# The row scalings of two layer norms moved from VectorE to ScalarE, in an attention and FFN block in float32

## The chip, the cores and the metric

One core of one Trainium2 chip runs the whole program. Its engines are TensorE (PE, matmuls into PSUM), VectorE (DVE), ScalarE (ACT), GpSimd (POOL) and SyncE (SP, which only issues transfers here). The metric is the time of one execution in device microseconds, the median over several. Lower is better.

## The reference, cut to what matters

```python
# x: (16, 16, 48, 128): 16 batches of 768 tokens with 128 channels, float32
def _ln(v, eps):                      # eps 1e-6 for the first norm, 1e-5 for the second
    m = jnp.mean(v, axis=-1, keepdims=True)
    s = jnp.var(v, axis=-1, keepdims=True)
    return (v - m) / jnp.sqrt(s + eps)

x = x + attention(_ln(x, 1e-6))       # 8 heads of 16, two relative position biases, causal in time, softmax over 768
t = x.reshape(16, 768, 128)
z = _ln(t, 1e-5)
top_p = top_k(softmax(z @ Wg), 2) / their_sum
for i in range(2):                    # every expert works on every token, scaled by top_p
    h = gelu(einsum("btd,edf->ebtf", z * top_p[..., i:i+1], W1) + b1)      # 8 experts, 512 wide
    out = out + einsum("ebtf,efd->btd", h, W2) + sum(b2)
x = t + out
```

## The kernel before, in words

A batch is 768 tokens, held as six tiles of 128 tokens (partitions) by 128 channels. For each batch the kernel computes the first norm, the transposes of its rows, query, key and value, the scores (twice: once for row maxima, once for the exponentials), the projection and residual, the second norm, the gate, and then the FFN.

The FFN is cut into 64 *units* a batch: 2 chunks of 384 tokens by 8 experts by 4 slices of the hidden width. A unit is a chain over all engines: three matmuls of TensorE into `zps` (L859 to L861), a product on VectorE (L691) that gives the second expert's input, two GELUs on ScalarE (L518 from PSUM, L519 from SBUF), the sum of both on GpSimd (L431), and six matmuls of TensorE into `acc` (L870). `zps` and `h0` have two buffers each. TensorE's matmuls of unit m wait for the first GELU of unit m - 2 (`h0_ready`), VectorE's product waits for the matmuls, and ScalarE's GELUs wait for the product (`z1_ready`).

The order of the work is written out by hand. `attention_plan` gives every attention step of the next batch a *slot* from 0 to 63; slots below 0 belong to the trip before. In slot k each engine does, in its own instruction order: the attention steps planned there; unit k + 4; what follows unit k (TensorE's matmuls into `acc`, at k = 63 VectorE's output addition). Units 60 to 63 of that count are units 0 to 3 of the next batch. Only for VectorE are the steps "stats", "seed", "root" and "scale" put at the end of their slot, behind the unit. The engines go through this list independently and meet at semaphores alone. The 64 slots are the body of one hardware loop with 15 trips; a last pass without attention follows, and a first attention without units stands ahead.

A norm is four kinds of steps, all on VectorE: "stats" (L589, row statistics of six tiles), "seed" (L595 to L601: moments and a first guess of 1 / sqrt), "root" (L605 to L608, one Newton step on 128x6 values, three times), and "scale" (L618): for each tile `xn = (x - mean) * ln_y`, with mean and ln_y one value a row. The first norm of a batch reads `x_in` and is scaled in two halves of three tiles, in slots 61 and 62 of trip b - 2 (trip f runs the units of batch f and the attention of batch f + 1); the second reads `xs` and is scaled whole in slot 54. TensorE then waits for `xn_ready` and transposes six tiles (L747, slot 0 or slot 56), ScalarE copies the result to `act_t` (L469), and from that come query and key (L752, L753) or the gate (L827). In slot 58 VectorE multiplies `xn` by the first gate weight (L665), and in slot 60 TensorE transposes again (L834).

Around the two places of the change ScalarE does, in order: unit 57, unit 58, unit 59, the copy L469, unit 60 (slots 53 to 56); and unit 0, unit 1, unit 2, unit 3 of the next batch, the loop's branch, the copy L469 (slots 60 to 64).

Of the kernel before, what the change touches and what calls it, by code (L numbers as in the profile page):

```python
# [9 lines left out]
ALU = mybir.AluOpType  # L10
ACT = mybir.ActivationFunctionType
AX = mybir.AxisListType

P = 128
# [4 lines left out]
TILES = TOK // P  # L19
# [7 lines left out]
HT = TILES // CHUNKS  # L27
# [52 lines left out]
WIDE = {(s, a): n for n, (s, a) in enumerate([(s, a) for _, s, a in PLAN if s in WIDE_STEPS])}  # L80
NARROW = {(s, a): n for n, (s, a) in enumerate([(s, a) for _, s, a in PLAN if s in NARROW_STEPS])}
assert len(WIDE) % 2 == 0
WPB = len(WIDE) // 2
NPB = len(NARROW)

VCHAIN = 2 * (5 + 3 * NEWTON) + 2
# [23 lines left out]
def build(nc, x, Wq, Wk, Wv, Wo, time_bias, part_bias, Wg, W1, b1, W2, b2, out):  # L110
    with ExitStack() as ctx:
        def sb(name, shape, dt=F32):
            return ctx.enter_context(nc.sbuf_tensor(name, shape, dt))
# [4 lines left out]
        def sem(name):  # L118
            return ctx.enter_context(nc.semaphore(name))
# [34 lines left out]
        ln_y = sb("ln_y", [P, TILES])  # L154
        ln_t = sb("ln_t", [P, TILES])
        sorted_l = halves[:, 3, QCOLS:QCOLS + 48].rearrange("p (i e) -> p i e", e=EXPERTS)
        gate_d = sb("gate_d", [P, TILES])
# [59 lines left out]
        x_loaded = sem("x_loaded")  # L217
        vec_chain = sem("vec_chain")
        xn_ready = sem("xn_ready")
        high_ready = sem("high_ready")  # L220
# [225 lines left out]
        def _(act):  # L446
# [16 lines left out]
            def attention(r, step, a):  # L463
                if step in WIDE_STEPS:
                    s, _, filled = wide_at(r, step, a)
                    w = wide[s]
                if step == "turn":
                    act.wait_ge(wide_filled[s], filled)
# [76 lines left out]
        def _(vec):  # L545
# [23 lines left out]
            def attention(r, step, a):  # L569
# [6 lines left out]
                if step in WIDE_STEPS:  # L576
                    s, _, filled = wide_at(r, step, a)
                    w = wide[s]
                if step in ("stats", "scale"):
                    src = x_in if a in (0, (0, 0), (0, 1)) else xs  # L580
                if step == "stats":
# [28 lines left out]
                elif step == "scale":  # L610
                    a, half = a
                    vec.wait_ge(vec_chain, r.at(VCHAIN, chain[0]))
                    if a == 0 and not (isinstance(r.b, int) and r.b == 0):
                        n = WIDE["split", 1]

                        vec.wait_ge(wide_filled[n % 2], r.at(WPB, n // 2 + 1 - WPB))
                    for i in range(half * HT, (half + 1) * HT):
                        ins = vec.tensor_scalar(xn[:, i, :], src[:, i, :], moments[:, i, 0:1], ln_y[:, i:i + 1],  # L618
                                                ALU.subtract, ALU.mult)
                    ins.then_inc(xn_ready, 1)  # L620
                elif step in ("query", "key"):
# [281 lines left out]
```

## Time and profile before

| | |
|---|---|
| median of 3 runs | 2642.08 us (2639.62 to 2646.99) |
| the profiled execution | 2641.69 us |
| its span, first to last instruction | 2639.8 us |
| mean granted TensorE clock | 0.961 |
| TensorE busy | 2334.7 us (88%) |
| ScalarE busy | 1653.6 us (63%) |
| VectorE busy | 1374.0 us (52%) |
| GpSimd busy | 1053.6 us (40%) |

Busy time is that of instructions on the engine; their overlap counts once. The granted clock is 1 at 2.4 GHz and 0.5 at 1.2 GHz. One trip of the loop takes 157.2 us. In a row, `h<-zps` means that the tile h is written from the tile zps; "idle before" is the time in which the engine stood still ahead of the instruction, with what ended it.

### The profile page before, as it was taken

How to read it: one execution, taken by the hardware profiler on the slowest of the kernel's cores; microseconds unless marked ns; L12 is line 12 of the kernel's file. 1: busy time of each engine (PE TensorE's matmuls, PEld its weight loads, DVE VectorE, ACT ScalarE, POOL GpSimd, SP SyncE). 2: the span in 40 equal slices, each digit the busy share in tenths (PEclk: the TensorE clock that was granted, in tenths of full speed). 3: DMA queues.
4: the chain of work that ended last, by engine and by line, in shares of the span. 5: the costliest groups of instructions: out<-in, count | busy, mean ns of one | idle time of the engine just before them, and what ended most of it. 6: DMA issues, size and time to landing. Idle time of an engine off the chain costs nothing.

```text
span 2639.8 us, 56828 instructions
## 1 busy us (share of the span) xinstructions
PE 2334.7 (88%) x18659; PEld 2093.4 (79%) x18659; DVE 1374.0 (52%) x3267; ACT 1653.6 (63%) x2760; POOL 1053.6 (40%) x1048
## 2 busy tenths in 40 slices
PE   1669989899998989999898998989999898998999
PEld 0458888787878878887887888878787887888888
DVE  2334474554636544573554547455463654447354
ACT  3227567576665757667566765757666566766767
POOL 1104344343534434353343434434352443434347
PEclk7679999999999999999999999999999999999999
DMA  3413022030212203022130212203022120302200
GB/s 47 78 39 41 10 33 27 11 48 9 29 25 30 30 8 49 10 27 27 18 42 7 38 16 33 27 11 46 10 27 27 27 32 8 47 11 29 27 10 7
DMA packets 70221, 71.26 MB, mean 27 GB/s; under 512 B 20462, under 2 KB 55242, under 8 KB 69962
## 3 DMA queue, kind: packets, MB, share of 16 engines
q1 hardware_dynamic: 69746, 67.64, 18.4%
q8 instruction: 173, 2.83, 0.4%
q14 instruction: 86, 0.70, 0.1%
q10 hardware_dynamic: 216, 0.08, 0.0%
HBM read 11.22 MB, written 6.29 MB: 7 GB/s over the span
## 4 chain that ended last, share of the span: by engine, by line
PE 62%; issue 13%; DVE 11%; ACT 8%; SPq 3%; DMA 1%; POOL 1%; DVEq 0%; ACTq 0%; POOLq 0%
PE acc L870 18%; PE zps L859 6%; PE narrow L800 6%; ACT z L490 5%; PE zps L861 5%; PE zps L860 5%; PE wide L769 5%; PE wide L784 5%; PE narrow L847 4%; DVE maxes L633 3%; DVE h L691 2%; PE wide L814 2%; PE wide L821 2%; PE wide L807 2%; DMA stack<-max_rows 1%
## 5 line engine op out<-in xcount | busy, mean ns | idle before, releaser
L431 POOL TENSOR_TENSOR hsum<-h 128x384 f32<-128x384 f32 x1024 | 1031.8, 1012 | 1499.3 <-ACT h L519 1463.9
L691 DVE TENSOR_TENSOR h<-zps,ratio_b 128x384 f32<-128x384 f32 x1024 | 562.9, 554 | 873.5 <-PE zps L861 870.8
L518 ACT ACTIVATE h<-zps,b_col 128x384 f32<-128x384 f32 x1024 | 594.6, 581 | 671.3 <-DVE h L691 640.7
L870 PE MATMUL acc<-w,hsum 128*128 128x128 f32 x6144 | 861.8, 277 | 1.5 <-DVE outt L700 1.2
L870 PEld LDWEIGHTS acc<-w,hsum 128*128 128x128 f32 x6144 | 844.2, 194 | 2.2 <-POOL hsum L431 1.7
L519 ACT ACTIVATE h<-h,b_col 128x384 f32<-128x384 f32 x1024 | 620.4, 606 | 0.0
L633 DVE TENSOR_REDUCE maxes<-wide 128x1 f32<-128x128 f32 (+5 forms) x768 | 438.5, 620 | 87.0 <-PE wide L769 83.2
L859 PE MATMUL zps<-x_hi,w_lo 128*128 128x384 f32 x1024 | 418.0, 408 | 59.3 <-ACT h L518 51.8
L490 ACT ACTIVATE z<-wide 128x896 f32<-128x896 f32 (+2 forms) x384 | 334.6, 916 | 41.0 <-PE wide L784 32.9
L861 PE MATMUL zps<-x_hi,w_hi 128*128 128x384 f32 x1024 | 351.0, 343 | 0.0
L860 PE MATMUL zps<-x_lo,w_hi 128*128 128x384 f32 x1024 | 350.6, 342 | 0.0
L784 PE MATMUL wide<-stack 128*128 128x256 f32 (+3 forms) x1280 | 256.6, 322 | 78.0 <-ACT z L490 45.1
L769 PE MATMUL wide<-stack 127*128 127x384 f32 (+2 forms) x1152 | 266.4, 346 | 41.6 <-DMA stack<-halves 38.0
L784 PEld LDWEIGHTS wide<-stack 128*128 128x128 f32 x1280 | 180.0, 192 | 148.0 <-ACT z L490 123.5
L859 PEld LDWEIGHTS zps<-x_hi,w_lo 128*128 128x128 f32 x1024 | 198.3, 194 | 92.5 <-ACT h L518 65.0
L769 PEld LDWEIGHTS wide<-stack 127*128 127x128 f32 x1152 | 181.8, 196 | 56.3 <-issue 40.4
L860 PEld LDWEIGHTS zps<-x_lo,w_hi 128*128 128x128 f32 x1024 | 199.3, 195 | 0.4
L861 PEld LDWEIGHTS zps<-x_hi,w_hi 128*128 128x128 f32 x1024 | 196.4, 192 | 0.0
L800 PE MATMUL narrow<-z,val 128*32 128x256 f32 (+3 forms) x2560 | 176.2, 394 | 3.3 <-ACT mixed L499 1.3
L800 PEld LDWEIGHTS narrow<-z,val 128*32 128x32 f32 x2560 | 83.2, 110 | 87.5 <-issue 22.0
L847 PE MATMUL narrow<-ident 128*128 128x128 f32 x1216 | 149.8, 282 | 0.0
L847 PEld LDWEIGHTS narrow<-ident 128*128 128x128 f32 x1216 | 144.4, 197 | 0.0
(91 smaller groups left out, 1343.2 us busy)
## 6 DMA issues: line engine op xcount, KB each, us to landing
stack<-halves SPq DMA_DIRECT2D x384, 96.0 KB, 3.0
stack<-halves SPq DMA_DIRECT2D x384, 24.0 KB, 2.7
x_in<-in_x SPq DMA_DIRECT2D x136, 48.0 KB, 2.4
out_dram<-outt SPq DMA_DIRECT2D x256, 24.0 KB, 1.7
w<-in_L_ffn_W SPq DMA_DIRECT2D x8, 256.0 KB, 4.4
stack<-max_rows SPq DMA_DIRECT2D x128, 3.0 KB
stack<-max_rows SPq DMA_DIRECT2D x128, 1.5 KB
stack<-z SPq DMA_DIRECT2D x6, 192.0 KB
```

What stands on the lines that cost most here:

```text
L431: pool.tensor_tensor(hsum[:, m % NHS, :], h0[:, m % 2, :], h1[:, m % NH1, :], ALU.add).then_inc(hsum_ready, 1)
L490: act.activation(z[:, hh, z0:z1], w[:, 0:z1 - z0], ACT.Exp).then_inc(wide_free[s], 1)
L518: act.activation(h0[:, m % 2, :], zps[m % 2][:, 0:CT], ACT.Gelu, bias=b1_col[:, j:j + 1]).then_inc(h0_ready, 1)
L519: act.activation(h1[:, m % NH1, :], h1[:, m % NH1, :], ACT.Gelu, bias=b1_col[:, j:j + 1]).then_inc(h1_ready, 1)
L633: ins = vec.tensor_reduce(maxes[:, hh * TILES + i:hh * TILES + i + 1], w[:, at:at + (i + 1) * P], AX.X, ALU.max)
L691: vec.tensor_tensor(h1[:, m % NH1, :], zps[m % 2][:, 0:CT], ratio_b[:, c * CT:(c + 1) * CT], ALU.mult).then_inc(z1_ready, 1)
L769: ins = pe.matmul(w[:, at:at + k1 - k0], qst[0:MAX_ROW, h, q0:q0 + P], kst[0:MAX_ROW, hh, k0:k1], start=True, stop=True)
L784: ins = pe.matmul(w[:, at:at + q1 - q0], kst[:, hh, i * P:(i + 1) * P], qst[:, g * GH + hh, q0 + shift:q1 + shift], start=True, stop=True)
L859: pe.matmul(zp, lo, x0_hi[:, cols], start=True, stop=False)
L860: pe.matmul(zp, hi, x0_lo[:, cols], start=False, stop=False)
L861: pe.matmul(zp, hi, x0_hi[:, cols], start=False, stop=True).then_inc(z_filled, 1)
L870: ins = pe.matmul(acc[:, n * P:(n + 1) * P], hsum[:, k % NHS, n * P:(n + 1) * P], w2[:, j, :], start=(j == 0 and n == 0), stop=(j == UNITS ...
```

## The change

ScalarE does the scaling as an Identity activation, `xn = ln_y * x + ln_b`, with a scale and a bias per row. VectorE computes the bias, `ln_b = -mean * ln_y`, one 128x6 operation ahead of the first half, and signals `shift_ready`; ScalarE waits for it. The twelve scalings a batch stand in the same slots, but on ScalarE they come at the slot's beginning, ahead of its unit.

```diff
--- before.py
+++ after.py
@@ -153,6 +153,7 @@
         ln_i = sb("ln_i", [P, TILES], I32)
         ln_y = sb("ln_y", [P, TILES])
         ln_t = sb("ln_t", [P, TILES])
+        ln_b = sb("ln_b", [P, TILES])
         sorted_l = halves[:, 3, QCOLS:QCOLS + 48].rearrange("p (i e) -> p i e", e=EXPERTS)
         gate_d = sb("gate_d", [P, TILES])
         gate_t = sb("gate_t", [P, TILES])
@@ -216,6 +217,7 @@
         sp_met = sem("sp_met")
         x_loaded = sem("x_loaded")
         vec_chain = sem("vec_chain")
+        shift_ready = sem("shift_ready")
         xn_ready = sem("xn_ready")
         high_ready = sem("high_ready")
         stack_loaded = [sem(f"stack_loaded{n}") for n in range(GH)]
@@ -464,7 +466,18 @@
                 if step in WIDE_STEPS:
                     s, _, filled = wide_at(r, step, a)
                     w = wide[s]
-                if step == "turn":
+                if step == "scale":
+                    a, half = a
+                    act.wait_ge(shift_ready, r.at(2, a + 1))
+                    if a == 0 and not (isinstance(r.b, int) and r.b == 0):
+                        n = WIDE["split", 1]
+
+                        act.wait_ge(wide_filled[n % 2], r.at(WPB, n // 2 + 1 - WPB))
+                    for i in range(half * HT, (half + 1) * HT):
+                        ins = act.activation(xn[:, i, :], (xs if a else x_in)[:, i, :], ACT.Identity, bias=ln_b[:, i:i + 1],
+                                             scale=ln_y[:, i:i + 1])
+                    ins.then_inc(xn_ready, 1)
+                elif step == "turn":
                     act.wait_ge(wide_filled[s], filled)
                     act.copy(act_t[:, :], w[:, 0:TOK]).then_inc(wide_free[s], 1)
                 elif step in ("query", "key"):
@@ -576,8 +589,8 @@
                 if step in WIDE_STEPS:
                     s, _, filled = wide_at(r, step, a)
                     w = wide[s]
-                if step in ("stats", "scale"):
-                    src = x_in if a in (0, (0, 0), (0, 1)) else xs
+                if step == "stats":
+                    src = x_in if a == 0 else xs
                 if step == "stats":
                     if a == 0:
                         chain[0] = 0
@@ -608,16 +621,10 @@
                     link(vec.scalar_tensor_tensor(out=ln_y[:, :], in0=ln_t[:, :], scalar=1.5, in1=ln_y[:, :],
                                                   op0=ALU.add, op1=ALU.mult))
                 elif step == "scale":
-                    a, half = a
-                    vec.wait_ge(vec_chain, r.at(VCHAIN, chain[0]))
-                    if a == 0 and not (isinstance(r.b, int) and r.b == 0):
-                        n = WIDE["split", 1]
-
-                        vec.wait_ge(wide_filled[n % 2], r.at(WPB, n // 2 + 1 - WPB))
-                    for i in range(half * HT, (half + 1) * HT):
-                        ins = vec.tensor_scalar(xn[:, i, :], src[:, i, :], moments[:, i, 0:1], ln_y[:, i:i + 1],
-                                                ALU.subtract, ALU.mult)
-                    ins.then_inc(xn_ready, 1)
+                    if a[1] == 0:
+                        vec.wait_ge(vec_chain, r.at(VCHAIN, chain[0]))
+                        vec.scalar_tensor_tensor(out=ln_b[:, :], in0=moments[:, :, 0], scalar=-1.0, in1=ln_y[:, :],
+                                                 op0=ALU.mult, op1=ALU.mult).then_inc(shift_ready, 1)
                 elif step in ("query", "key"):
                     n, scale = (0, HD ** -0.5) if step == "query" else (2, 1.0)
                     vec.wait_ge(high_ready, r.at(2, 1 + n // 2))
```

## Rows read from the trace of the kernel before

**Rows 1.** The page's chain that ended last, by engine, and busy time.

```profile
PE 2334.7 (88%) x18659; PEld 2093.4 (79%) x18659; DVE 1374.0 (52%) x3267; ACT 1653.6 (63%) x2760; POOL 1053.6 (40%) x1048
...
PE 62%; issue 13%; DVE 11%; ACT 8%; SPq 3%; DMA 1%; POOL 1%; DVEq 0%; ACTq 0%; POOLq 0%
```

**Rows 2.** The waits; us in total, times, longest us.

```profile
PE zps L859 <- ACT h L518: 51.8, 46, 5.8
...
PE wide L747 <- issue: 35.2, 14, 2.8
```

**Rows 3.** Timeline of TensorE, place A; start, us, instruction, idle before.

```profile
1142.86 0.44 PE L859 MATMUL zps<-x_hi,w_lo 128*128 128x384 f32 x1 [1.30 <-ACT h L518]
...
1143.49 0.83 PE L870 MATMUL acc<-w,hsum 128*128 128x128 f32 x6
...
1146.70 0.87 PE L747 MATMUL wide<-ident,xn 128*128 128x128 f32 x6 [2.38 <-issue]
```

**Rows 4.** Timeline of VectorE, place A.

```profile
1141.41 0.17 DVE L608 SCALAR_TENSOR_TENSOR ln_y<-ln_t,ln_y 128x6 f32<-128x6 f32 x1
1141.58 0.56 DVE L691 TENSOR_TENSOR h<-zps,ratio_b 128x384 f32<-128x384 f32 x1
1142.05 0.85 DVE L618 TENSOR_SCALAR xn<-x_in,moments,ln_y 128x128 f32<-128x128 f32 x3
...
1143.28 1.54 DVE L618 TENSOR_SCALAR xn<-x_in,moments,ln_y 128x128 f32<-128x128 f32 x3
```

**Rows 5.** Timeline of VectorE, place B.

```profile
1122.10 3.00 DVE L618 TENSOR_SCALAR xn<-xs,moments,ln_y 128x128 f32<-128x128 f32 x6
```

**Rows 6.** Timeline of ScalarE, place B.

```profile
1121.80 0.58 ACT L518 ACTIVATE h<-zps,b_col 128x384 f32<-128x384 f32 x1 [0.55 <-DVE h L691]
...
1122.78 0.57 ACT L518 ACTIVATE h<-zps,b_col 128x384 f32<-128x384 f32 x1
...
1125.66 0.58 ACT L518 ACTIVATE h<-zps,b_col 128x384 f32<-128x384 f32 x1 [1.80 <-DVE h L691]
...
1126.65 0.79 ACT L469 COPY act_t<-wide 128x768 f32<-128x768 f32 x1
```

**Rows 7.** Timeline of TensorE, place B.

```profile
1127.49 1.50 PE L827 MATMUL narrow<-wg,act_t 128*128 128x8 f32 x12 [0.21 <-ACT act_t L469]
```

**Rows 8.** ScalarE's groups by line and shape; busy us, mean ns | idle before.

```profile
L519 ACT ACTIVATE h<-h,b_col 128x384 f32<-128x384 f32 x1024 | 620.4, 606 | 0.0
L518 ACT ACTIVATE h<-zps,b_col 128x384 f32<-128x384 f32 x1024 | 594.6, 581 | 671.3 <-DVE h L691 640.7 <-POOL hsum L431 12.0
L490 ACT ACTIVATE z<-wide 128x1024 f32<-128x1024 f32 x128 | 131.2, 1025 | 32.0 <-PE wide L784 24.2
...
L490 ACT ACTIVATE z<-wide 128x768 f32<-128x768 f32 x128 | 103.7, 811 | 0.9 <-PE wide L784 0.9
...
L490 ACT ACT_TABLE_LOAD x30 | 38.5, 1283 | 0.5
...
L510 ACT COPY ratio_b<-wide 128x384 f32<-128x384 f32 x32 | 16.1, 503 | 0.0
...
L459 ACT COPY b_row<-acc 128x128 f32<-128x128 f32 x1 | 0.3, 266 | 0.4 <-PE acc L715 0.4
```

**Rows 9.** Timeline of ScalarE, place A.

```profile
1142.23 0.58 ACT L518 ACTIVATE h<-zps,b_col 128x384 f32<-128x384 f32 x1 [1.96 <-DVE h L691]
...
1147.61 0.80 ACT L469 COPY act_t<-wide 128x768 f32<-128x768 f32 x1 [1.14 <-PE wide L747]
```

**Rows 10.** Chain that ended last, the first 60 us; start, us, what.

```profile
39.35 3.77 SPq L324
```

**Rows 11.** Timeline of VectorE, batch 0's second norm, ahead of the loop.

```profile
177.80 1.63 DVE L618 TENSOR_SCALAR xn<-xs,moments,ln_y 128x128 f32<-128x128 f32 x6
```

**Rows 12.** Windows round place A; PE, PEld, DVE, ACT, POOL busy, PEclk, DMA share, GB/s.

```profile
982.80:998.80 16.00, 11.97 (x63) 10.53 (x63) 8.40 (x19) 8.08 (x14) 6.14 (x6) 0.79 0.08 15
1140.00:1156.00 16.00, 12.32 (x69) 10.88 (x68) 9.25 (x20) 8.12 (x14) 6.13 (x6) 0.89 0.07 15
```

## The prediction

> **What bounds the kernel now.** I read the page first: TensorE is busy 88% of the span, ScalarE 63%, VectorE 52%, and the chain that ended last is 62% PE, with 13% issue, 11% DVE and 8% ACT [rows 1]. So most of the time TensorE's own work sets the pace, and a change to ScalarE or VectorE counts only where TensorE waits for one of them. The waits say where that is [rows 2]: 46 times for a GELU (L518), and 14 times before the transposes of L747 for nothing the profile shows ("issue", 2.5 us each). The timeline then shows where such waits meet the scalings: in two places of every batch (period 157.2 us; I work with the batch that ends near 1145 us).
>
> *Place A, the end of the loop body* (slots 61 to 63, first norm of the batch after next). TensorE waits 1.30 us for unit 1's GELU, then runs unit 3 and the last six matmuls into acc until 1144.32, and then stands still 2.38 us until the transposes L747 [rows 3]. VectorE finished the second half of the rows at 1143.28 + 1.54 = 1144.82 [rows 4], 1.88 us before they are used. The rest of the pause is the loop's branch: the transposes are the first TensorE work of the next trip.
>
> *Place B, slots 53 to 57* (second norm). VectorE writes six tiles in 3.00 us [rows 5]. It alone also holds up its next product, so ScalarE's next GELU starts at 1125.66 after 1.80 us of idleness, the copy of the transposed rows (L469) at 1126.65, and TensorE's gate matmuls wait for exactly that copy, at 1127.49 [rows 6, 7].
>
> **The change part by part.**
>
> *What one scaling costs on ScalarE.* No row has a 128x128 activation from SBUF with a scale and a bias per row. The nearest is the GELU L519, 128x384 from SBUF with a bias per row, 606 ns. The slope is (1025 - 811) / 256 = 0.84 ns per element (the two Exp rows), so 256 elements fewer is 214 ns less: 392 ns. A per-row operand more is the difference between L518 (581 ns, PSUM, bias) and the copy L510 (503 ns, PSUM, no row operand): 78 ns. That gives 470 ns [rows 8]. Activations overlap: one unit is 581 + 606 = 1187 ns of duration but takes 0.98 us from start to start (1121.80 to 1122.78) [rows 6], so each overlaps its neighbour by 0.10 us. I take c = 0.37 us per tile from start to start. The lower bound is the plain copy of 128x128, 266 ns [rows 8], less 0.10: c = 0.17. The upper is L519 itself: c = 0.50.
>
> *Place A.* ScalarE gets three activations in slot 61 ahead of unit 1 and three in slot 62 ahead of unit 2; it had idled before unit 1 only because it waited for VectorE's product. Now: VectorE's product starts at 1141.58, its next instruction 0.47 us later at 1142.05 [rows 4]. That next one is now the row shift ln_b, a 128x6 operation; I take 0.17 us for it, as its neighbours of that shape (end 1142.22), and 0.09 us from VectorE's end to ScalarE's start, as at unit 1 (1141.58 + 0.56 = 1142.14 to 1142.23) [rows 4, 9]. ScalarE starts scaling at 1142.31 and unit 1 at 1142.31 + 3c. Before, it was 1142.23 [rows 9]. Hence 0.08 + 3c = 1.19 us later (0.59 to 1.58). TensorE's unit m waits for the GELU of unit m - 2, since its result lands where that one reads; so unit 3 waited for just this GELU, and all behind it moves with it: unit 3, the matmuls into acc, the branch, the transposes. The 1.88 us in which the rows lay ready do not hide it, because it is not the rows that come late but the GELU that stands behind them on ScalarE. The second half: unit 1 takes 0.98, so scaling starts at 1144.48 and ends at 1145.7; TensorE needs it at 1147.9, hidden. Units 2 and 3 then end at 1147.7, and the copy L469 can follow 1.14 us later or sooner, since that is all the idleness it had [rows 9], that is at 1148.8; the transposes end at 1146.70 + 0.87 + 1.19 = 1148.8. No cost, but no cover left either: each 0.1 us more shows there. VectorE's six tiles go, but its product of unit 3 waits for TensorE anyway: no gain at A.
>
> *Place B.* ScalarE cannot begin before unit 57's GELUs are issued, 1122.78 [rows 6]. ln_b comes after VectorE's product, at 1122.10 where the first tile started [rows 5]; if GpSimd's addition holds it up it is ready by some 1122.6, so its wait costs nothing. What now stands behind the six tiles on ScalarE is unit 58, which used to run beside VectorE's scaling, then unit 59, then the copy: 1122.78 + 6c + 2 x 0.98 = 1124.74 + 6c, against 1126.65. So 6c - 1.91 = +0.31 us (-0.89 to +1.09). The rows themselves are ready at 1125.1, as before. TensorE's gate matmuls move by this, and behind them in a fixed sequence VectorE's top 2, the weights, the split.
>
> *Start.* The first norm now stands behind the long casts on ScalarE (to 26.9), but from there the chain runs through SP's transfers of the bias rows, 12 issues one after the other like the one in [rows 10]: nothing. Batch 0's second norm runs with no units beside it: VectorE took 1.63 us for six tiles [rows 11]; now 0.26 + 5c + 0.47 = 2.58, +0.95 us. The next first norm there adds about 0.5 in the same way. Together 1.4 us (-0.5 to 2.7).
>
> *Sum.* A batch costs (0.08 + 3c) + (6c - 1.91) = 9c - 1.83 = 1.50 us; times 15 trips 22.5; with the start 23.9 us.
>
> *The clock.* Right after place A TensorE's granted clock falls. Over 16 us round it the mean is 0.79 in 10 of the 15 trips, which is 0.21 x 16 / 0.5 = 6.7 us at 1.2 GHz; in 4 it is 0.89, 3.5 us; in the last 1.00. One of each of the first two stands in [rows 12]. The fall follows TensorE's pauses of 1.30 and 2.38 us. The first becomes 2.5 us. If the clock then falls before unit 3 instead of after, unit 3 and the matmuls into acc (1142.86 to 1144.32, 1.46 us) take twice as long. Ends: 0 and 14 x 1.46 = 20 us; I take a quarter, 5 us.
>
> Total: the profiled execution has 2641.69 us (span 2639.8 and 1.9 around it), 0.4 under the median of 2642.08. 2641.7 + 23.9 + 5 = 2670.6; I say 2670.
>
> **Two rules of the Trainium skill.** L618's six tiles take 1.63 us at the start, where GpSimd is idle, and 3.00 us at place B, where it adds [rows 5, 11]. The Trainium skill, page "SBUF — State Buffer", section on the engine ports, says VectorE in its two-port modes and GpSimd lock each other out of one port pair, while ScalarE waits for nobody; by that rule the move should save the 1.37 us lost. The trace agrees that VectorE loses time there, but at B the rows become ready no sooner, as ScalarE is free only at 1122.78.
> The activation's price can also be had from "ScalarE: Activation LUTs", section "What ACT_TABLE_LOAD costs": 186 ns + 0.833 per element, 93 more for each per-row operand, 93 of overlap. That would be c = 0.386 and an estimate of 24.7 us for 15 trips in place of 22.5.
>
> **The rivals.**
> *R1, ScalarE is cheap and the lock goes (not slower).* Place B decides. If c is near the plain copy's 0.17, the chain at B gets 0.89 us shorter (VectorE no longer stands 3.00 us in front of its product and ScalarE's GELU), A loses 0.59, and the trip gains 0.30: 2641.7 - 4.5 - 0.5 = 2637. It decides below c = 1.83 / 9 = 0.20 us. For it: VectorE's tiles at B cost nearly double what they cost alone. Against it: L519 takes 606 ns for 384 elements, and no slope in the rows brings a two-operand activation to 0.27.
> *R2, the clock.* The low stretch starts earlier at each of 14 trips (+20) and in some lasts longer too: 2641.7 + 23.9 + 20 = 2686, to 2705. For it: 14 of 15 trips already fall, with less idleness. Against: the fall may come no sooner, since unit 3 lies between the two pauses.
> *R3, table loads.* If Identity isn't in the GELU's table, each of the three places (slots 54, 61, 62) brings two loads of 1.283 us [rows 8]: 7.7 us a trip, 115 in all, some 2780. Against it: copies (L469, L510) run between GELUs without a load, the 31 loads before L518 and 30 before L490 are about what the turns from Exp to GELU and back need (two of each a batch).
> That the trace of before shows Identity free of loads I can't say; "ScalarE: Activation LUTs", section "Table sets", names it as a filler of every set, which speaks against R3.
> *R4, place A is absorbed.* If the branch can run while TensorE waits for the GELU, part of 1.19 us is hidden; with B alone 2641.7 + 15 x 0.31 + 1.4 = 2648. Against: the matmuls into acc stand between the wait and the branch.
>
> **How the numbers follow.** A measurement of this kernel tells some 0.3% (7.9 us) from no change, so "same" is 2634 to 2650. Forecast 0.62 (2655 to 2682, from c = 0.30 to 0.42 and the clock at 0 to 10 us); R2 0.18; R1 0.11, of which 0.04 beyond 0.3% faster; R4 0.06, nearly all inside 0.3%; R3 0.03. Faster 0.04, same 0.13, slower 0.83. The bounds c = 0.17 and 0.50 with the clock at 0 and 20 give 2637 and 2705; leaving out R1, R3 and the far end of R2, 2 in 10, the range is 2646 to 2694.
>
> **What would show it.** In the profile after: L618's place taken by ScalarE activations of about 0.47 us, 0.37 apart (c wrong otherwise). At A: TensorE's wait for ScalarE before unit 3 about 2.5 us instead of 1.30, the pause before the transposes still about 2.4. At B: copy L469 and the gate 0.3 us later relative to unit 57. Period 158.7 us plus the clock's share. Table loads still 62. The forecast is wrong if the period doesn't grow, if the pause before the transposes shrinks by what the wait grew, or if the clock's low stretches grow by more than a third.

## The result, and the profile after

The changed kernel takes 2684.44 us (median of 4 runs, 2679.76 to 2689.48) against 2641.65 us (4 runs, 2639.62 to 2646.99) of the kernel before on the same chip: ratio 1.0159, 95% interval 1.0134 to 1.0184, 42.8 us slower. The forecast was 2670 us, 28 us slower. The profiled execution has a span of 2680.6 us, 40.8 us longer.

The page of the changed kernel, busy times and the chain that ended last by engine; ScalarE has gained busy time, VectorE lost it, and the chain has moved 2 points to ScalarE ([rows 1] before):

```profile
PE 2367.9 (88%) x18659; PEld 2125.0 (79%) x18659; DVE 1308.9 (49%) x3102; ACT 1725.9 (64%) x2958; POOL 1052.3 (39%) x1048
...
PE 62%; DVE 12%; issue 10%; ACT 10%; SPq 3%; DMA 1%; POOL 0%; DVEq 0%; ACTq 0%; POOLq 0%
```

ScalarE's groups by line and shape. The scalings take 0.48 us each (estimated 0.47), and there are 31 and 30 table loads, as before ([rows 8] has the 30 of L490): R3 is out.

```profile
L477 ACT ACTIVATE xn<-x_in,ln_b,ln_y 128x128 f32<-128x128 f32 x102 | 42.5, 482 | 36.3 <-DVE ln_b L626 36.3
L531 ACT ACT_TABLE_LOAD x31 | 39.8, 1283 | 13.3 <-DVE h L698 11.7
L477 ACT ACTIVATE xn<-xs,ln_b,ln_y 128x128 f32<-128x128 f32 x96 | 38.5, 481 | 16.0 <-DVE ln_b L626 16.0
L503 ACT ACT_TABLE_LOAD x30 | 38.5, 1283 | 0.5
```

Place A in the batch that ends near 1160 us, TensorE's timeline. From the start of unit 2 (1151.73) to unit 3 it is 3.98 us; before it was 1142.86 - 1140.12 = 2.74, from this row to that in [rows 3]:

```profile
1140.12 0.42 PE L859 MATMUL zps<-x_hi,w_lo 128*128 128x384 f32 x1
```

The wait for ScalarE has gone from 1.30 to 2.54 us ([rows 3]), and unit 3 and the matmuls into acc (L877) run at 1.2 GHz in this trip: 1.49 us against 0.83 for the latter.

```profile
1151.73 0.42 PE L866 MATMUL zps<-x_hi,w_lo 128*128 128x384 f32 x1
...
1155.71 0.69 PE L866 MATMUL zps<-x_hi,w_lo 128*128 128x384 f32 x1 [2.54 <-ACT h L531]
...
1156.83 1.49 PE L877 MATMUL acc<-w,hsum 128*128 128x128 f32 x6
...
1160.13 1.53 PE L754 MATMUL wide<-ident,xn 128*128 128x128 f32 x6 [1.81 <-issue]
```

The slower matmuls do not make the transposes later. Two other trips of the changed kernel, rows of unit 3 and of the transposes; in the first unit 3 and the matmuls into acc run at 2.4 GHz and end 1.46 us after unit 3's start, in the second at 1.2 GHz and end after 2.61 us. The transposes start 3.95 and 3.78 us after unit 3; the pause at the loop's branch is shorter by about what the matmuls took longer.

```profile
1473.64 0.44 PE L866 MATMUL zps<-x_hi,w_lo 128*128 128x384 f32 x1 [2.54 <-ACT h L531]
...
1477.59 1.54 PE L754 MATMUL wide<-ident,xn 128*128 128x128 f32 x6 [2.49 <-issue]
```

```profile
1315.97 0.69 PE L866 MATMUL zps<-x_hi,w_lo 128*128 128x384 f32 x1 [2.54 <-ACT h L531]
...
1319.75 1.54 PE L754 MATMUL wide<-ident,xn 128*128 128x128 f32 x6 [1.16 <-issue]
```

The same on ScalarE as in the first rows of place A: three scalings stand in front of unit 1's GELU, which starts at 1155.10, 1.17 us after the first of them. The last row is the copy of the transposed rows, with 2.44 us of idleness before it (1.9 to 2.5 in all trips but the first): cover that the forecast hadn't seen.

```profile
1153.93 1.26 ACT L477 ACTIVATE xn<-x_in,ln_b,ln_y 128x128 f32<-128x128 f32 x3 [2.05 <-DVE ln_b L626]
1155.10 0.56 ACT L531 ACTIVATE h<-zps,b_col 128x384 f32<-128x384 f32 x1
...
1161.70 0.80 ACT L482 COPY act_t<-wide 128x768 f32<-128x768 f32 x1 [2.44 <-PE wide L754]
```

Place B on ScalarE. Unit 57 starts at 1133.03, the scalings at 1134.02, unit 58 at 1136.33, the copy at 1138.26: 5.23 us from unit 57 to the copy, against 1126.65 - 1121.80 = 4.85 ([rows 6]).

```profile
1133.03 0.58 ACT L531 ACTIVATE h<-zps,b_col 128x384 f32<-128x384 f32 x1 [0.55 <-DVE h L698]
...
1134.02 2.41 ACT L477 ACTIVATE xn<-xs,ln_b,ln_y 128x128 f32<-128x128 f32 x6
1136.33 0.57 ACT L531 ACTIVATE h<-zps,b_col 128x384 f32<-128x384 f32 x1
...
1138.26 0.79 ACT L482 COPY act_t<-wide 128x768 f32<-128x768 f32 x1
```

Windows of the changed kernel (engines' busy times in the order PE, PEld, DVE, ACT, POOL, then granted clock, DMA share, GB/s), the first in the scores of the second head group, the second at place A. Before, only the first trip had a stretch at a low clock in the scores; of the changed kernel's trips 2 to 15 nine have one or two.

```profile
1099.00:1108.00 9.00, 8.47 (x35) 5.57 (x39) 0.00 (x0) 7.17 (x8) 0.00 (x0) 0.62 0.00 0
1155.00:1166.00 11.00, 8.48 (x34) 8.15 (x35) 2.90 (x5) 6.59 (x14) 4.27 (x4) 0.53 0.12 25
```

To see where the 40.8 us lie I took, from the timelines of every kernel, the starts of the two transposes of each trip (L747 before, L754 after), and the low-clock time between them (the share of the granted clock below 1, times the length, times two). "B to A" runs from the transposes of the second norm, "A to B" from those of the first. The low-clock time stands in three parts: from B to A; in the first 14 us behind the transposes at A; and in the rest of A to B, which holds the scores. Means over trips 2 to 15, us (the first trip has 17 to 19 us of low clock from B to A in every kernel):

| kernel | median us | trip | B to A | A to B | low, B to A | low, first 14 us of A to B | low, rest of A to B |
|---|---|---|---|---|---|---|---|
| before | 2642 | 157.0 | 21.6 | 135.4 | 1.4 | 4.4 | 0.0 |
| changed | 2684 | 159.9 | 23.2 | 136.7 | 3.6 | 5.0 | 4.6 |
| e1, only A moved | 2679 | 159.4 | 23.1 | 136.3 | 3.3 | 4.5 | 3.7 |
| e2, only B moved | 2669 | 158.2 | 22.2 | 136.0 | 0.2 | 3.5 | 3.4 |
| e3, A behind the unit | 2664 | 158.6 | 22.1 | 136.5 | 0.1 | 3.6 | 5.6 |
| e4, B split | 2642 | 157.0 | 22.0 | 135.0 | 1.7 | 5.1 | 1.7 |
| e5, changed + 20 spare | 2680 | 159.5 | 23.9 | 135.6 | 0.0 | 0.2 | 7.8 |
| e6, changed + spare in the scores | 2769 | 165.7 | 23.4 | 142.3 | 3.6 | 7.5 | 0.2 |
| e7, split + spare in the scores | 2734 | 163.5 | 22.0 | 141.5 | 1.4 | 8.0 | 0.1 |
| e8, second half doubled | 2693 | 159.7 | 23.3 | 136.4 | 3.6 | 4.7 | 3.9 |
| e9, changed + 10 spare | 2683 | 159.6 | 23.3 | 136.3 | 0.8 | 4.0 | 3.0 |
| e10, before + 5 spare | 2643 | 157.0 | 21.6 | 135.4 | 0.0 | 2.9 | 3.4 |
| e11, split + 5 spare | 2636 | 156.5 | 21.9 | 134.6 | 0.2 | 1.9 | 5.5 |
| e12, before + delay at B | 2666 | 158.2 | 22.7 | 135.6 | 3.0 | 4.0 | 1.5 |

The columns come from the profiled execution alone; the medians from all runs. From B to A the change costs 1.58 us in each of trips 2 to 15: 0.32 from the transposes at B to the start of unit 2, 1.24 from there to unit 3, 0.02 from unit 3 to the transposes at A. Added up over all 15 trips it is 22.7 us from B to A (the first trip gains only 0.45), 14.7 us from A to B, where nothing was moved, 1.5 us ahead of the loop (batch 0's transposes start at 181.05 against 179.57) and 1.9 us behind the last trip. That is the 40.8.

What a microsecond of low clock costs depends on where it lies, and single trips of one profile tell it. Three kinds of trips of e11, one window for each (columns as above): no low clock at all, 3.4 us of it right behind the transposes, and 13.7 us of it in the scores:

```profile
1129.40:1283.50 154.10, 143.05 (x1176) 128.78 (x1177) 83.44 (x200) 102.73 (x176) 64.20 (x64) 1.00 0.19 26
1594.30:1750.20 155.90, 144.55 (x1176) 130.20 (x1176) 83.48 (x200) 102.85 (x176) 64.18 (x64) 0.99 0.18 26
815.20:972.30 157.10, 147.62 (x1176) 133.11 (x1176) 83.39 (x200) 103.08 (x176) 64.17 (x64) 0.96 0.18 25
```

e11 has four trips of the first kind, three of the second and three of the third; from A to B they take 132.4, 134.0 and 135.4 us on average. So the time right behind the transposes costs 0.47 us a microsecond, that in the scores 0.22. The kernel before gives 0.45 for the first (134.9 us in the trips with 3.4 us, 135.6 in those with 4.9), e2 and e3 give 0.24 for the second. From B to A the trips of the kernel before, and those of the changed one, are nearly equally long with more and with less low clock, for the reason just seen at place A. By these prices the changed kernel's A to B should be 4.6 x 0.24 + 0.5 x 0.45 = 1.3 us longer in trips 2 to 15; it is 1.29.

### The profile page after: what moved, and what is told of

It is laid out like the page before. It is cut to its first block, busy times and chain, and to the rows that moved or that the text cites. A ratio compares the mean times of both kernels' runs of the same rounds, so it can differ in the third digit from the quotient of the medians.

```text
span 2680.6 us, 56891 instructions
## 1 busy us (share of the span) xinstructions
PE 2367.9 (88%) x18659; PEld 2125.0 (79%) x18659; DVE 1308.9 (49%) x3102; ACT 1725.9 (64%) x2958; POOL 1052.3 (39%) x1048
## 3 DMA queue, kind: packets, MB, share of 16 engines
q14 instruction: 156, 1.28, 0.2%
## 4 chain that ended last, share of the span: by engine, by line
PE 62%; DVE 12%; issue 10%; ACT 10%; SPq 3%; DMA 1%; POOL 0%; DVEq 0%; ACTq 0%; POOLq 0%
PE acc L877 18%; PE narrow L807 6%; PE zps L866 6%; PE wide L791 5%; PE zps L868 5%; PE zps L867 5%; ACT z L503 5%; PE wide L776 4%; PE narrow L854 4%; DVE maxes L640 3%; ACT xn L477 2%; PE wide L828 2%; PE wide L821 2%; DVE h L698 2%; PE wide L814 1%
## 5 line engine op out<-in xcount | busy, mean ns | idle before, releaser
L877 PE MATMUL acc<-w,hsum 128*128 128x128 f32 x6144 | 872.1, 279 | 0.6 <-POOL hsum L433 0.2
L877 PEld LDWEIGHTS acc<-w,hsum 128*128 128x128 f32 x6144 | 853.6, 196 | 1.3 <-issue 0.9
L791 PE MATMUL wide<-stack 128*128 128x256 f32 (+3 forms) x1280 | 268.7, 338 | 74.5 <-ACT z L503 43.7
L791 PEld LDWEIGHTS wide<-stack 128*128 128x128 f32 x1280 | 192.7, 206 | 142.9 <-ACT z L503 118.6
```

Of the source, the lines that this page charges most:

```text
L791: ins = pe.matmul(w[:, at:at + q1 - q0], kst[:, hh, i * P:(i + 1) * P], qst[:, g * GH + hh, q0 + shift:q1 + shift], start=True, stop=True)
L877: ins = pe.matmul(acc[:, n * P:(n + 1) * P], hsum[:, k % NHS, n * P:(n + 1) * P], w2[:, j, :], start=(j == 0 and n == 0), stop=(j == UNITS ...
```

## The experiments

Theory when the experiments began: ScalarE does the scalings in front of GELUs for which TensorE waits (24 us), and the rest is TensorE's clock, which falls because of the longer pause at place A. Rival: the rest is load, on ScalarE or from VectorE's side. The diffs are against the changed kernel unless said otherwise.

**e1 and e2: one norm alone.** `ON_ACT` names the halves on ScalarE; the others are done by VectorE in its old place.

```diff
+ON_ACT = ((0, 0), (0, 1))      # e1;  e2: ((1, 0), (1, 1))
...
                 if step == "scale":
+                    if a not in ON_ACT:
+                        return
...
+                    if a not in ON_ACT:
...
+                        for i in range(half * HT, (half + 1) * HT):
+                            ins = vec.tensor_scalar(xn[:, i, :], (xs if a else x_in)[:, i, :], moments[:, i, 0:1],
+                                                    ln_y[:, i:i + 1], ALU.subtract, ALU.mult)
```

> Only the first norm's six scalings (place A, slots 61 and 62) are on ScalarE; the second norm's stay on VectorE. Theory (order on ScalarE plus clock): unit 3 comes 1.24 us later a trip, 18.6 us, the start 0.5; with it comes most of the extra low-clock time, since the pause before unit 3 is 2.5 instead of 1.3 us: time 2665 to 2680, low-clock time of the profile well above 105 us (150 or more). Rival (the rest is no matter of the clock but of ScalarE's or VectorE's load, half of it each place): 2642 + 19 + 8 = 2669 with low-clock time near 105 us.

> Only the second norm's six scalings (place B, slot 54) are on ScalarE. Theory: 0.38 us a trip and 1 at the start, 6.7 us, with the pause before unit 3 unchanged at 1.30 us: 2649, and low-clock time within 15 us of 105. Rival (load, no clock): 2642 + 6.7 + 8 = 2657 with unchanged low-clock time.

Measured: e1 2679.3 us (2675.26 to 2682.96), ratio to before 1.0142, interval 1.0127 to 1.0156. e2 2668.8 us, ratio 1.0104 (1.0078 to 1.0129), with runs from 2655.38 to 2678.49. e1 fits the theory (2665 to 2680, low-clock time 182 us from 200 us on). e2 missed both numbers, 2649 and 2657: place B is 25 us, not 7, though its low-clock time in the profiled run (one of the two fastest of six) is 112 us from 200 us on, close to the 102 of before. B to A is 0.6 us longer, where the copy explains 0.38; TensorE also waits longer for VectorE's x_lo at the split, in e2 and e1 11.2 and 11.3 us in 15 waits, before and in the changed kernel 7.4 and 7.3 (first the wait of before, then that of e2):

```profile
PE zps L859 <- DVE x_lo L670: 7.4, 15, 0.5
```

```profile
PE zps L881 <- DVE x_lo L692: 11.2, 15, 0.8
```

That is 0.25 us a trip, and it is not in the changed kernel; why it comes up in e1 and e2 is open. It is a part of why the single places don't add up to the whole (36 + 26 against 43). What else e2 shows is in single trips. Windows of e2: a trip of 160.3 us, an undisturbed one of 157.1, and two stretches in the scores of the first; then the same places in the scores of the second:

```profile
974.50:1134.80 160.30, 148.04 (x1166) 133.59 (x1166) 82.82 (x197) 104.38 (x179) 64.20 (x64) 0.95 0.18 25
1455.30:1612.40 157.10, 143.57 (x1166) 129.26 (x1167) 82.82 (x197) 104.05 (x179) 64.21 (x64) 0.99 0.18 25
1048.00:1055.00 7.00, 6.85 (x27) 5.99 (x26) 0.56 (x1) 5.43 (x7) 0.00 (x0) 0.51 0.75 94
1099.00:1107.00 8.00, 7.82 (x40) 5.10 (x44) 0.00 (x0) 5.41 (x7) 0.00 (x0) 0.57 0.00 0
```

```profile
1530.00:1538.00 8.00, 7.42 (x70) 1.00 0.70 89
1581.00:1589.00 8.00, 7.74 (x89) 1.00 0.01 2
```

The number of instructions and the work of VectorE, ScalarE and GpSimd are the same; 3.2 us more where TensorE runs the scores at 1.2 GHz. 4 of e2's trips 2 to 15 are such, the other ten take 156.9 to 158.3. So the clock costs time in the scores, far from both places of the change. The spread of e2's runs is the same thing: two runs with a mean granted clock of 0.959 take 2655.4 and 2659.5 us, three with 0.943 or 0.944 take 2673.9 to 2678.5. That is 83 us more of low clock and 19 us more of time, 0.23 for one, as in the single trips.

**e3: the same activations, behind the unit.** ScalarE does the first norm's halves at the end of slots 61 and 62.

```diff
-                        if slot + start == k and (step in last) == late:
+                        if slot + start == k and (step in last or (step, a) in last) == late:
...
-            rounds(act, attention, unit, lambda r, k: None, prepare=prepare)
+            rounds(act, attention, unit, lambda r, k: None, last=(('scale', (0, 0)), ('scale', (0, 1))), prepare=prepare)
```

> As the changed kernel, but ScalarE does the first norm's halves at the end of slots 61 and 62, behind units 1 and 2. Theory: unit 1's GELU is no longer late, so the pause before unit 3 is 1.30 us again, and 1.24 x 15 = 18.6 us go. The second half is ready at about the time of the transposes (1146.5 against 1146.7 in the batch of before), and unit 3's GELUs end 1 us later than before, so copy L482 may come up to 1 us late: 2684 less 18.6 less the clock's share (5 to 17) = 2649 to 2661, up to 2670 if the copy is late. Rival (it is the load, not the order): 2680 or more.

Measured: 2664.0 us (2657.01 to 2670.42), ratio 1.0082 (1.0067 to 1.0096), 20 us less than the changed kernel and above the 2649 to 2661 expected; the up to 2670 for a late copy covers it, but the copy was not late (see below). TensorE's timeline: the pause before unit 3 is back at 1.30, and the transposes come 3.97 us after unit 3's start, 3.84 before (4.15 against 3.97 on average); it is the rows that end that pause now, so what comes late is the transposes, by 0.17 us.

```profile
1473.44 0.44 PE L866 MATMUL zps<-x_hi,w_lo 128*128 128x384 f32 x1 [1.30 <-ACT h L531]
...
1477.41 0.89 PE L754 MATMUL wide<-ident,xn 128*128 128x128 f32 x6 [2.51 <-ACT xn L477]
```

The number of activations is the same, only their order isn't, and B to A is 1.1 us a trip shorter than in the changed kernel: the load rival falls, the order is the cause at place A. A to B is not shorter (136.5 against 136.7): seven of e3's trips have low clock in the scores, though the pause before unit 3 is as short as before. So that pause is not what brings those stretches.

**e4: three tiles to each engine at B,** the first norm on VectorE (`ON_ACT = ((1, 1),)`).

> Three of the second norm's tiles on ScalarE, three on VectorE at the same time; all else as in the kernel before (the first norm on VectorE). Theory (c = 0.385, order on ScalarE decides): the copy of the transposed rows can start at 1122.78 + 3 x 0.385 + 2 x 0.98 = 1125.9 instead of 1126.65, 0.75 us earlier a trip: 2642 - 11 = 2631, with the clock's share 2626 to 2637. Rival (the wait for the rows decides, not the GELUs): no change, 2642 or more.

Measured: 2642.27 us (2637.66 to 2644.23), ratio 0.9994 (0.9985 to 1.0003): no change, outside the theory's 2626 to 2637, as the rival said, but for another reason. ScalarE's timeline shows the gain at its place: from unit 57 to the copy 1440.89 - 1436.82 = 4.07 us, 0.78 less than before.

```profile
1436.82 0.58 ACT L535 ACTIVATE h<-zps,b_col 128x384 f32<-128x384 f32 x1 [0.55 <-DVE h L713]
...
1437.80 1.25 ACT L481 ACTIVATE xn<-xs,ln_b,ln_y 128x128 f32<-128x128 f32 x3
1438.96 0.56 ACT L535 ACTIVATE h<-zps,b_col 128x384 f32<-128x384 f32 x1
...
1440.89 0.79 ACT L486 COPY act_t<-wide 128x768 f32<-128x768 f32 x1
```

The trip is as long as before (157.0 us) with 2.6 us more of low clock. A trip with 5 us behind the transposes and none in the scores takes 156.4 to 156.8 us, against 157.0 to 157.5 before; but seven of the trips have 3.4 us more in the scores and take 157.2 to 157.6. The clock has taken the gain.

**e5, e9 and e10: spare matmuls in the pause before unit 3,** 20 and 10 in the changed kernel, 5 in the kernel before; their results are not used.

```diff
+                if m == 3:
+                    idle(r, ("mix", (0, 0)), 20, NPB)      # e9: 10;  e10, e11: 5
 
                 pe.wait_ge(h0_ready, r.at(UNITS, m + 1))
```

> As the changed kernel, with 20 spare 128x128 matmuls (2.1 us, as those of L854, their result unused) on TensorE between unit 2 and its wait for unit 3, so that the 2.54 us pause becomes some 0.4. Theory (part of the loss is the clock, and that pause brings it): the stretches at 1.2 GHz at place A go back from 7 to 10 us a trip to the 3.4 to 6.8 of before; low-clock time falls from 204 us by 30 to 80, the time by 7 to 19: 2666 to 2678. Rival (the serial order alone): 2684 as the changed kernel.

> As the changed kernel, with 10 spare matmuls of 128x128 between unit 2 and unit 3 (each issues as two, 2.3 us in all; the 20 tried before took 4.63 us, more than the 2.54 us pause, and delayed unit 3 by some 2 us). Theory (the pause brings the low clock at place A): no stretch at 1.2 GHz from place A in most trips, B to A 22.9 us as before or less, A to B 133.5 us plus 0.23 times the low-clock time left in the scores: 2655 to 2668, low-clock time 130 or less. Rival (the serial order alone): 2684.

> As the kernel before, with 5 such matmuls (1.2 us) in its 1.30 us pause ahead of unit 3. Theory: its low-clock stretches at place A (3.4 to 6.8 us in 14 trips) go, at 0.23 to 0.3 us each: 1 to 2 us a trip, 2613 to 2630; if instead stretches in the scores come up, as in the two kernels with another trip length, up to 2645. Rival (the pause at the branch, 2.4 us, brings them, not the one before unit 3): 2643.

Measured: e5 2680.0 us (2666.68 to 2688.36), e9 2683.1 us (2674.56 to 2685.96), ratios 1.0133 (1.0112 to 1.0154) and 1.0148 (1.013 to 1.0167); e10 2643.2 us (2636.06 to 2648.78), ratio 1.0002 (0.9992 to 1.0012). All three missed the theory's ranges (2666 to 2678, 2655 to 2668, 2613 to 2630); e10 fits the alternative it named, stretches in the scores, up to 2645. The 20 calls were sized wrongly: they issue as 40 and take 4.63 us, more than the pause. But they did hold the clock at place A, as TensorE's timeline and the window there show (TensorE alone ahead of the window with all engines):

```profile
1155.10 4.63 PE L854 MATMUL narrow<-ident 128*128 128x128 f32 x40
1159.49 0.42 PE L868 MATMUL zps<-x_hi,w_lo 128*128 128x384 f32 x1
...
1162.28 0.87 PE L754 MATMUL wide<-ident,xn 128*128 128x128 f32 x6 [1.36 <-issue]
```

```profile
1155.00:1166.00 11.00, 9.18 (x76) 8.80 (x74) 3.32 (x9) 6.16 (x13) 3.07 (x4) 1.00 0.09 17
```

The right size, e9, filled the pause without delaying unit 3:

```profile
1471.34 2.40 PE L854 MATMUL narrow<-ident 128*128 128x128 f32 x20
1474.05 0.45 PE L868 MATMUL zps<-x_hi,w_lo 128*128 128x384 f32 x1 [0.31 <-ACT h L531]
```

Its low-clock time is 122 us from 190 us on against 204, and the time is that of the changed kernel within 2 us, as the rival said. But that does not mean that the low clock costs nothing. Half of what went lay from B to A, where it is free. From A to B the 15 trips are 5.0 us shorter than in the changed kernel; from B to A they are 4.9 longer, 3.0 of it in the first trip, where there was no pause to fill. e5 shows the same more strongly: hardly any low clock is left behind the transposes and A to B is 15.8 us shorter over the 15 trips, though the scores have 3.2 us more of low clock a trip; the fill, too long, gives back 15.4 us from B to A. And in e10 the fill took 1.5 us a trip away behind the transposes and the scores got 3.4 us: at 0.45 and 0.22 that is even, and the time did not move.

So my theory (the pause before unit 3 brings the low clock that is paid for) holds in part for the stretch right behind the transposes, which costs the kernel before nearly as much as the changed one (4.4 and 5.0 us a trip) and explains little of the difference between them. It fails for the stretches in the scores, which come up whether that pause is filled or not.

**e6 and e7: spare matmuls in the scores,** three in each later part, in the changed kernel and in the split kernel.

```diff
                     if hh == 0 and part == 1:
                         idle(r, ("mix", (g, 0)), 13)
+                    elif hh:
+                        idle(r, ("mix", (g, 0)), 3)
```

> As the changed kernel, with three spare matmuls more in each of the nine later parts of the scores of both head groups, where TensorE waits some 0.5 us a part for ScalarE's Exp. Theory: these pauses bring the low-clock stretches that stand in the trace of the changed kernel about 36 and 90 us before place B and hardly in the one before; they go, 60 to 80 us of low-clock time, at 0.23 us each: 2684 - 14 to 18 = 2666 to 2670. Rival (these stretches cost nothing, TensorE waits there anyway, or the fillers delay the Exp): 2684 or more.

> Second norm split three tiles to each engine, first norm on VectorE (the split kernel, 2642), with the same spare matmuls in the scores. The split kernel's trip is 0.7 us shorter once the low-clock time is taken out, but has 2.6 us more of it a trip, in the scores. Theory: with these gone the 0.7 us shows: 2642 - 15 x 0.6 = 2633, range 2626 to 2638, faster than the kernel before. Rival (the trip is held by something else): 2642.

Measured: 2768.8 us (2765.63 to 2771.52) and 2734.5 us (2733.95 to 2739.01), 84 and 92 us more than without. The low clock in the scores did go (0.2 and 0.1 us a trip left), but the spare matmuls, 245 us of work for TensorE over the run, fitted its pauses only in part: 84 us of them came on top. They hide whatever the low stretches cost, so this experiment can't say.

**e8: the second half's work doubled.**

```diff
+                    for i in range(HT) if (a, half) == (0, 1) else ():
+                        act.activation(spare[:, i, :], x_in[:, i, :], ACT.Identity, bias=ln_b[:, i:i + 1],
+                                       scale=ln_y[:, i:i + 1])
```

> As the changed kernel, with three more activations of 128x128 (into a spare tile, results unused) ahead of the second half's three in slot 62: 1.15 us more work for ScalarE a trip there. What the prediction said (no cover left behind units 2 and 3 and the loop's branch): up to 1.1 us a trip, 2684 + 16 = 2700. Rival, from the trace of the changed kernel, where ScalarE idles 2.44 us before the copy L482: all of it hidden, 2684 within 5.

Measured: 2693.0 us (2683.7 to 2694.07), 8.6 above the changed kernel, between both expectations. Yet B to A is 23.3 us (23.2 without), and ScalarE still idles 1.03 us before the copy in this trip:

```profile
1168.78 0.80 ACT L486 COPY act_t<-wide 128x768 f32<-128x768 f32 x1 [1.03 <-PE wide L758]
```

At its place the added 1.15 us is hidden: ScalarE idles 0.6 to 1.3 us there in all trips but the first, against 1.9 to 2.5 in the changed kernel. Of the profiled run's 6.7 us more, 2.5 lie ahead of the loop and in the first trip, where nothing covers the work, 1.9 behind the last trip, and 2.4 in the other trips. The rest of the 8.6 us in the median is not explained.

**e11: the split and the 5 spare matmuls together.**

> Second norm's tiles split three and three, first norm on VectorE, and the 5 spare matmuls ahead of unit 3. Theory: 0.7 us a trip less than the kernel before with the same matmuls, 10 us: 2603 to 2635. Rival: the time of the kernel before with the matmuls, within 4 us, since what the split saves goes to the clock.

Measured: 2636.2 us (2628.63 to 2640.62), ratio 0.9975 (0.9963 to 0.9986): 0.25% faster than the kernel before, the only version that is. It is 7.0 us below e10 on the same chip, so here most of the split's gain (10 us expected) came through; the time lies just above the theory's range and 3 us below the rival's. Its four trips without any low clock take 154.0 to 154.7 us, those with the most 160.2. Neither part alone gave it (e4, e10).

**e12: the delay by itself.** In the kernel before, nothing moved, two spare activations ahead of the second norm's copy.

```diff
                 if step == "turn":
+                    for n in range(2) if a else ():
+                        act.activation(spare[:, n, :], ident[:, :], ACT.Identity, bias=b1_col[:, 0:1], scale=b1_col[:, 1:2])
                     act.wait_ge(wide_filled[s], filled)
```

> The kernel before, with nothing moved, and two spare 128x128 activations (0.77 us) on ScalarE right ahead of the second norm's copy of the transposed rows: the disputed delay by itself, of the size that the kernel with only the second norm's scalings moved has (0.6 to 0.7 us a trip from B to A). Theory (a small delay there is partly taken up by the clock's stretches and partly brings new ones in the scores in some trips, whatever its cause): undisturbed trips of 157.1 us as in the kernel before, a few of 158 to 161 with 7 us or more of low clock in the scores, time 2650 to 2675. Rival (moving the scalings does something else too): the plain sum 2643 + 11 = 2654 with every trip longer by the same 0.7 us and none with a new stretch.

Measured: 2665.5 us (2659.2 to 2667.29), ratio 1.0079 (1.0065 to 1.0093), 22.4 us more for 15 x 0.77 = 11.6 us of work:

```profile
1288.78 0.87 ACT L470 ACTIVATE spare<-ident,b_col 128x128 f32<-128x128 f32 x2
1289.55 0.78 ACT L472 COPY act_t<-wide 128x768 f32<-128x768 f32 x1
```

Trips 2 to 15 range from 157.0 to 160.1 us, with 12.9 us of low clock from A to B in the longest. B to A grew by 1.1 us, 0.3 more than was put in: in ten trips a low stretch now starts ahead of unit 2, where the kernel before has none, and there unit 2 comes 0.28 us later than in the others. The profiled run is the fastest of the five (clock 0.955, 17.5 us over the profile of before); the three slowest have 0.947 or 0.948. So a delay on this chain costs 1.5 to 2 times itself, whoever causes it: e2's 25 us for 0.6 us a trip needs nothing that is special to the scalings.

## Why the prediction was right or wrong

*The price of a scaling.* Forecast 0.47 us, 0.37 apart; measured 0.48, and six of them in 2.41 us, 0.386 apart. R1 needed 0.20: it fell by that. The estimate from the Trainium skill's page "ScalarE: Activation LUTs", section "What ACT_TABLE_LOAD costs", 0.386, was the exact one; mine from the rows was 4% low, since the copy's and the GELU's difference gave 78 ns for a row operand.

*Place A.* Forecast +1.19, measured +1.24; e3 shows that the order does it, e1 that this place by itself makes most of the loss (36 of 43 us). R4 had the branch absorb part of the wait for the GELU; it didn't, the transposes come as long after unit 3 as before (3.99 against 3.97 us on average). What the forecast had wrong is the cover behind it: it gave the copy none, and there is 1.9 to 2.5 us (and e8 used it). It had read 1.14 us off a trip of the kernel before that is one of three such; the other eleven have 1.8 to 2.3.

*Place B.* Forecast +0.31, measured +0.38 at the copy and +0.32 up to unit 2. As a cost of the whole kernel it is another matter: e2 gave 25 us.

*Sum of both.* 1.50 us a trip forecast from B to A, 1.58 measured there, and 1.4 against 1.5 ahead of the loop. Over the run that is 22.7 and 1.5, 24.2 us, against 23.9 forecast. This part was right in mechanism and size.

*The shared port.* GpSimd still lengthens VectorE's operations: in both kernels one 128x6 operation of each Newton step (L606 before, L619 after, 99 in all) takes 38.8 us over the run; single ones take 0.97 us instead of 0.17 where GpSimd's addition runs beside it. The 1.37 us that six tiles lost to it at B bought nothing, as said, because ScalarE was busy until then.

*The clock.* This is the term that was off: 5 us forecast, and 42.8 less 24.2 = 18.6 left over by the runs, 14.7 of it from A to B in the profiled one. The forecast's own sign for it came true: it would be wrong, it said, if the low stretches grew by more than a third, and the low-clock time of the profile grew from 205 to 303 us, by 48%. Two steps failed. The first is what was priced: unit 3 and the matmuls into acc at half speed, 0 to 1.46 us a trip. They did run slower in 11 of trips 2 to 15, at full length (2.61 against 1.46 us) in eight, but the transposes came no later for it (4.00 us after unit 3 in those eight, 3.99 in the three at full clock), so this costs nothing. The second is what was left out: the scores had no place in the sum. There the changed kernel has 4.6 us of low clock a trip and the kernel before none, at 0.24 us each. R2 came nearest in time (2686), by the same mistaken price. That 2684 lies inside the stated range is therefore in part luck: the place and its cost that the range allowed for were not those that were paid.

How sure this is: the price of low clock in the scores is shown by trips of one kernel against each other (e2, e3, e11, the changed kernel) and by runs of one kernel against each other (e2), which agree at 0.22 to 0.24, and the sum comes out; no experiment took the stretches away at no cost, as e6 and e7 were to do. Why a longer trip meets more of them is open.

## What to carry to other kernels

Before moving work to an idle engine, ask what stands behind it in that engine's order: ScalarE was idle 37% of the time, and yet three activations cost their full 1.2 us because they stood in front of the one GELU that TensorE waited for; behind it (e3) they cost 0.2 us at that place. Split work between two engines that are free at the same moment rather than move it (e4, e11). And where TensorE's clock falls in some trips, count on a delay on the critical chain costing up to twice itself (e12), and on a gain vanishing (e4). Read the loss from trips of one profile against each other, and price low clock by its place: ahead of a pause that is there anyway it is free, over dense work it is not. A fill that leaves the time as it was may have gained there and lost beside it (e5, e9).

## What the runs showed of the hardware

- A microsecond at 1.2 GHz costs about 0.45 us right behind the transposes at A (kernel before, e11), 0.22 to 0.24 in the scores (e2, e3, e11), and nothing between unit 3 and the loop's branch.
- Trips without a stretch in the scores have nearly the same length in the kernel before (156.3 to 157.5 us), in e2 and in e3 (156.9 to 157.5, one of e2's 158.3), although B to A differs by 0.6 us between them; the low stretch after place A took up the difference (low clock is 3.4 us in most of e2's and e3's undisturbed trips, 6.8 in most of the kernel before). A small change can so vanish, or cost twice.
- The pause at the loop's branch is not a fixed length added to the work ahead of it: the transposes start 3.8 to 4.4 us after unit 3 in the changed kernel, whether the matmuls between take 1.46 or 2.61 us. With spare matmuls queued ahead of unit 3 (e5) it is 2.8 to 3.4 us, and the pause 1.36 instead of 2.4 in the trip shown.
- 20 calls of a float32 128x128 matmul issue as 40 instructions and take 4.63 us; 10 calls took 2.40, 5 calls 1.28.
